# The fp6 layers' residual sum moves from VectorE to TensorE, and its copy out of PSUM to ScalarE

## The reference, cut to what matters

```python
x = x + 0.5 * _L1_ffn_ref(_layernorm(x, axis=-1), L1_ffn_weight, L1_ffn_bias)

# _L1_ffn_ref:
xq, xs = _mx_quantize(x2)          # blocks of 32 features share a scale; values go to the nearest of the fp6 grid
wq, ws = _mx_quantize(w2)
xd = (xq * xs[..., None]).reshape(x2.shape)
wd = (wq * ws[..., None]).reshape(w2.shape)
out = xd @ wd.T + bias
```

## Time and profile before

| what | value |
|---|---|
| median of three runs | 2520.27 us (2518.9 to 2527.7) |
| the profiled execution, its own time | 2511.65 us |
| span of its trace | 2509.8 us |
| TensorE, VectorE, ScalarE busy | 84%, 61%, 39% of the span |
| mean granted clock of TensorE | 0.916 |
| first fp6 stage | until 1623 us of the span |
| last fp6 stage | about 2408 to 2505 us |

### The profile page before, as it was taken

How to read it: one execution, slowest core, us unless ns; L and a number is a source line. 1 busy time by engine, 2 the same in 40 slices (tenths; PEclk the granted TensorE clock), 3 DMA queues, 4 the chain that set the end, 5 groups by cost and what they waited for, 6 DMA issues and landing times.

```text
span 2509.8 us, 38629 instructions
## 1 busy us (share of the span) xinstructions
PE 2113.4 (84%) x12842; PEld 1582.3 (63%) x12842; DVE 1519.2 (61%) x4411; ACT 970.8 (39%) x1961; POOL 319.6 (13%) x298
## 2 busy tenths in 40 slices
PE   5589999967999964899999647678998998999957
PEld 3478888855888944788888525524554554554446
DVE  7744344346555577444334498677777676777368
ACT  4122332222333342223233234325555555555643
POOL 4320000022000043300000252311001101100000
PEclk8799999988999997999999856769999999999976
DMA  8120101111000031200110130342242242242002
GB/s 264 43 65 25 31 27 31 31 51 40 1 1 1 1 110 45 72 25 27 31 31 27 54 92 7 75 53 58 40 53 53 52 52 52 53 52 28 2 9 67
DMA packets 84035, 114.83 MB, mean 46 GB/s; under 512 B 12212, under 2 KB 73816, under 8 KB 80728
## 3 DMA queue, kind: packets, MB, share of 16 engines
q1 hardware_dynamic: 77416, 94.80, 17.2%
q0 software_dynamic: 6432, 17.57, 2.2%
HBM read 69.16 MB, written 43.17 MB: 45 GB/s over the span
## 4 chain that ended last, share of the span: by engine, by line
PE 61%; DVE 26%; ACT 5%; issue 4%; DMA 2%; POOL 2%; DVEq 0%; ACTq 0%; SPq 0%; POOLq 0%
PE psum L775 10%; PE psum L777 10%; PE psum L776 10%; PE psum L126 5%; PE psum L2289 4%; PE psum L128 4%; PE psum L127 4%; DVE mt L2177 4%; PE psum L2268 3%; PE psum L862 3%; DVE m L2165 2%; PE psum L2248 2%; DVE m L2174 2%; DVE stats L160 2%; DVE xn L185 2%
## 5 line engine op out<-in xcount | busy, mean ns | idle before, releaser
L2128 ACT ACTIVATE pt<-psum 128x512 f32<-128x512 f32 (+3 forms) x768 | 333.7, 492 | 274.5 <-DVE psum L2203 180.7
L740 DVE SCALAR_TENSOR_TENSOR h<-psum,xg,sg 128x128 f32<-128x128 f32 x592 | 166.8, 344 | 415.4 <-PE psum L862 415.4
L556 ACT ACTIVATE sg<-psum 128x512 f32<-128x512 f32 x180 | 107.7, 598 | 573.8 <-PE psum L777 573.8
L775 PE MATMUL psum<-w_hi,xt_hi 128*128 (+1 forms) x720 | 285.1, 396 | 33.7 <-DVE xt_lo L705 33.7
L776 PE MATMUL psum<-w_lo,xt_hi 128*128 (+1 forms) x720 | 283.3, 393 | 0.0
L777 PE MATMUL psum<-w_hi,xt_lo 128*128 (+1 forms) x720 | 283.1, 393 | 0.0
L2248 PE MATMUL psum<-ks,qs 96*128 96x512 bf16 (+3 forms) x768 | 235.2, 346 | 34.3 <-DMA ks<-qk_scr 9.0
L2268 PE MATMUL psum<-qs,ks 99*128 99x512 bf16 (+3 forms) x768 | 238.7, 334 | 24.5 <-ACT pt L2128 18.8
L775 PE MATMUL psum<-w_hi,ht_hi 128*128 (+1 forms) x720 | 218.1, 303 | 0.2
L2272 PE MATMUL psum<-band,ident_r 128*128 128x256 f32 (+1 forms) x864 | 215.7, 338 | 0.0
L2177 DVE CUSTOM_DVE_ANT_0 mt<-psum,band_q 128x256 bf16<-128x256 f32 (+1 forms) x512 | 204.7, 400 | 17.3 <-PE psum L2248 7.1
(11 more groups left out here) (283 smaller groups left out, 4377.6 us busy)
## 6 DMA issues: line engine op xcount, KB each, us to landing
xg<-w_dram SPq DMA_DIRECT2D x54, 256.0 KB, 3.2
qk_scr<-parts SPq DMA_DIRECT2D x32, 384.0 KB, 2.5
qs<-qk_scr SPq DMA_DIRECT2D x96, 128.0 KB, 7.1
ks<-qk_scr SPq DMA_DIRECT2D x96, 128.0 KB, 7.7
xg<-rows_in SPq DMA_DIRECT2D x74, 132.0 KB, 2.1
rows_out<-yb SPq DMA_DIRECT2D x74, 128.0 KB, 1.7
x<-x_dram SPq DMA_DIRECT2D x4, 1024.0 KB, 8.5
out_dram<-x SPq DMA_DIRECT2D x4, 1024.0 KB, 4.5
```

What stands on the lines that cost most here:

```text
L740: ins = dve.scalar_tensor_tensor(out=h[i % 2][:, e, :], in0=u[:, e, :], scalar=xg[j % XSLOT][:, at:at + 1], in1=sg[i % 2][:, e, :], op0=AL ...
L775: pe.matmul(out, a[0], b[0], start=first, stop=False)
L2128: act.activation(pt[n % NPT][:, 0:q1 - q0], st_bank(n)[:, 0:q1 - q0], ACT.Exp).then_inc(*exped.up())
```

## The change

TensorE opens the accumulation of each tile with a matmul of the 128x128 identity by the tile of `X`, both in plain 32 bits, so that the residual is in the sum. The weight's two parts are halved as they are copied out of PSUM, and so is the row of ones that multiplies the bias. The sum in PSUM is then the new x, and ScalarE copies it into `X`, where VectorE had multiplied and added. The step `sum` keeps its place in the order and changes its engine.

```diff
+        W_SCALE = 0.5
...
-                    pool.memset(minus[:, :], -1.0).then_inc(*S("ones").up())
+                    pool.memset(minus[:, :], -W_SCALE).then_inc(*S("ones").up())
...
-                            act.activation(wt[0][:, c, :], ring.bank((kind, c))[:, 0:D],
-                                           ACT.Copy).then_inc(*wt_hi.up())
+                            act.activation(wt[0][:, c, :], ring.bank((kind, c))[:, 0:D], ACT.Copy,
+                                           scale=W_SCALE).then_inc(*wt_hi.up())
...
+                        elif kind == "sum":
+                            act.wait_ge(*lin(c + 1))
+                            act.activation(flat(X[:, c * TILES:(c + 1) * TILES, :]), ring.bank(("lin", c)),
+                                           ACT.Copy).then_inc(*lin_x.up())
...
-                            dve.tensor_tensor(wt[1][:, c, :], ring.bank((kind, c))[:, 0:D],
-                                              wt[0][:, c, :].bitcast(F32), ALU.subtract).then_inc(*wt_lo.up())
+                            dve.scalar_tensor_tensor(out=wt[1][:, c, :], in0=ring.bank((kind, c))[:, 0:D], scalar=W_SCALE,
+                                                     in1=wt[0][:, c, :].bitcast(F32), op0=ALU.mult,
+                                                     op1=ALU.subtract).then_inc(*wt_lo.up())
...
-                        elif kind == "sum":
-                            dve.wait_ge(*lin(c + 1))
-                            dst = flat(X[:, c * TILES:(c + 1) * TILES, :])
-                            dve.scalar_tensor_tensor(out=dst, in0=ring.bank(("lin", c)), scalar=0.5, in1=dst,
-                                                     op0=ALU.mult, op1=ALU.add).then_inc(*lin_x.up())
...
-                                pe.matmul(o, ones[:, :], bias_2[:, :], start=True, stop=False)
+                                pe.matmul(o, ident[:, :], X[:, c * TILES + t, :], start=True, stop=False)
+                                pe.matmul(o, ones[:, :], bias_2[:, :], start=False, stop=False)
```

## The result

The changed kernel takes 2531.2 us at the median of 20 runs (2522.8 to 2539.8), the kernel before 2520.1 us (2509.6 to 2529.1). The ratio is 1.0044, with an interval of 1.0029 to 1.0058: slower by 11 us, where +22 was forecast. The time lies in the forecast range; the size is half of it. The profiled execution took 2532.42 us, 20.8 more than that of before, so the profiled pair and the medians disagree by 10 us. That difference was the first thing to explain.

The account below looks back on a forecast made before the run. The prediction took TensorE at a mixed clock to become the last stage's bound, in place of VectorE and TensorE loops of nearly equal length. Last stage +11.3 and first +11.0 made +22.3 on the median 2520.3: 2543 us, range 2516 to 2572.

Parts of the forecast that it names:

- Sum: ... = +11.0 us: First fp6 stage: the terms of quads 0 to 7 and the stage's end together add 11.0 us.
- a first stage that ends within 4 us of its old time: First fp6 stage: a sign that the prediction, which added 11.0 us there, is wrong.
- the terms for quads 4 to 7 and the end: First stage after 1540 us: quads 4 and 6 +2.2 each, quad 5 +1.5, quad 7 +3.4, end +2.8.
- VectorE's wait for ScalarE's sums: First stage, quad 1: the longer product makes VectorE wait in the `collect` needing the sum, net +1.0 us (0.5 to 1.7).
- +11.3 us: Last fp6 stage: six quads at a mixed clock add 7.8 us, the last two quads 3.5.
- 12.0 us per quad: Last stage: TensorE bounds, its clock rising 7.5 us after a product's start; 12.0 us per quad against 10.70.
- The VectorE loop of a quad becomes 10.38 - 1.20 = 9.2 us: Last stage: without the two sums, 1.20 us on the chain, VectorE's loop per quad falls to 9.2 us.
- I take nothing: Last stage: ScalarE's added copy is covered by TensorE's transposes and costs nothing, 0.15 us at most per quad.
- The price of a product: Both fp6 stages: each identity product costs TensorE 0.44 us at the full clock, 0.86 at the half.
- The sum on the median: Whole kernel: +22.3 us, worked out on the profiled execution's 2511.65, is added to the median 2520.3.
- Rival B: Both fp6 stages: denser products hold the clock at 2.4 GHz, VectorE's saving decides; total -6, 2514 us; chance 0.12.
- Rival C: Both fp6 stages: the clock stays low throughout, 14.45 us per quad in the last; total +56, 2576 us; chance 0.15.

Follow-up runs that it names:

- first_only: The change in the first fp6 stage alone (TensorE adds twice the residual, ScalarE halves the sum), against the kernel before: ratio 1.0022 (1.0001 to 1.0043).
- before_third: The kernel before, unchanged, run once more for a third trace: 2527.1 us.
- last_only: The change in the last fp6 stage alone (TensorE adds twice the residual, ScalarE halves the sum), against the kernel before: ratio 1.0043 (1.0026 to 1.0060).
- after_full: The changed kernel with the bias product's two rows widened to 128 by zeros: ratio 0.9977 (0.9960 to 0.9995) to the kernel before.
- after_full_swap: The changed kernel with the bias product widened to 128 rows and, on VectorE, next quad's `scaled` ahead of this one's `even`: 2506.8 us, 0.9946 to the kernel before.
- no_ident: The changed kernel without the identity products, ScalarE still copying the sum: ratio 1.0021 (1.0003 to 1.0039) to the kernel before.
- double: The changed kernel with each identity product issued twice, counting the residual twice: ratio 1.0058 (1.0039 to 1.0077) to the kernel before.

## Why the prediction was wrong

It had the direction and the kind of loss; the size was twice what was measured. Point by point:

- *The first stage, "Sum: ... = +11.0 us", is the term that was mis-sized.* The traces give 3.7 us between the means, in a spread of 9 within the same code, and `first_only` 5.5 with an interval that ends short of 11. The forecast had named a first stage that ends within 4 us of its old time as a sign of being wrong; between the means it is met (the profiled pair has 4.9 us in length, 4.4 in its end). What failed is the part after 1540 us: the terms for quads 4 to 7 and the end, +12.1 in all. From quad 4's product to the end of the stage the four traces without the change took 64.3, 67.8, 71.1 and 72.2 us, the three with it 68.7, 69.7 and 69.7: +0.5 between the means. The terms took the clock of one execution, the shortest, as given and added the new products to it. From quad 4's product to quad 7's in the profiled execution of before, in `before_third` and in the changed kernel:

```profile
1559.10:1611.90 52.80, 39.74 (x195) 32.19 (x195) 37.39 (x65) 23.41 (x41) 15.60 (x10) 0.82 0.15 51
1561.70:1621.00 59.30, 46.07 (x195) 37.18 (x194) 37.34 (x65) 23.37 (x41) 15.58 (x10) 0.70 0.13 45
1559.10:1614.60 55.50, 43.69 (x220) 33.09 (x218) 33.73 (x59) 26.16 (x47) 16.24 (x11) 0.90 0.14 49
```

  From the first to the start of the last matmul, quads 4 and 6 took 5.3 and 5.4 us in the profiled execution, mostly at the upper clock, but 8.0 and 8.0 at the lower in `before_third` and `last_only`. With the change they took 7.0 to 7.1 and 6.6 in all three traces: 1.7 and 1.1 us more than in the execution shown, for the 2.2 priced, and less than in those two. Quad 7 was priced at +3.4 because its product ran at the half clock. In the profiled execution of the changed kernel:

```profile
1614.59 0.97 PE psum L1531 x2
...
1617.64 0.79 PE psum L1531 x2
...
1619.65 0.43 PE psum L1531 x2
...
1621.30 0.43 PE psum L1531 x2
...
1624.40 0.60 ACT v L1834
```

  The last tiles' products step by 0.43: the clock had risen, and the product took as long as without the added work, 1614.6 to about 1623 us against 1611.9 to 1620.3. In the other two traces it took 2.3 us more than before. Over the stage from its first bias DMA to its end the mean granted clock is 0.66, 0.63, 0.63 and 0.61 in the four traces without the change, 0.74, 0.70 and 0.70 in those with it. The other way, from the first product to quad 4's the stage took 77.4 us on the mean for 74.2, +3.2 where the terms had -1.0. There VectorE's wait for ScalarE's sums was priced for one quad; in the whole stage it came in four, 21.5 us with 10.5 at most, where before VectorE waited 7.3 us for the products in its sums. The end of the stage was right: 2.6 us for the 2.8 priced.
- *The last stage, "+11.3 us"*: measured 11.0 between the means of all traces, 10.8 by `last_only`. Here the total was right and its inside was not, so that it came out is in part luck. "12.0 us per quad" is the mean of the first six (13.7, 10.6, 13.3, 10.5, 13.3, 10.7), but by alternation: the clock rose only with the end of a slow quad's product, some 11 us after its start and not 7.5, and then held for one whole quad. The last two quads took 13.3 and 7.5, which is 8 more than in the profiled execution and 1 to 5 more than in the other three traces, for the 3.5 priced.
- *"The VectorE loop of a quad becomes 10.38 - 1.20 = 9.2 us" failed.* With TensorE out of the way (`after_full`) the loop was 10.5. Of the 1.2 us, 0.9 went to the wait for ScalarE's `sizes`, which the sums had covered; `after_full_swap` takes that wait away and gets 9.8 in its best quads.
- *"I take nothing" for ScalarE's copy failed.* I asked what it delays behind TensorE and not what it delays behind the `sizes`. `no_ident` puts the whole move at +5 us (ratio 1.0003 to 1.0039); how much of it is the copy alone was not measured.
- *The price of a product*, 0.44 and 0.86 us, was right: tiles of 2.94 us at the half clock, and in `double` 2.08 at the full, 0.44 over the changed kernel's 1.64.
- *The sum on the median.* I added a difference worked out on the profiled execution to a median 8.6 us above it. That execution had the shortest first and last stage of the four. Against it the changed kernel's profiled execution lost 16.1 us in the last stage and 4.9 in the first, 21.0 together, close to the 22.3 forecast but with both terms wrong in opposite directions. The median lost 11: part of the 22 is what other executions of the kernel before lose by themselves.
- *Rival B* did not occur, but `double` shows its mechanism a step away: there the upper clock held across the transposes and the gap of every quad, so what the prediction reads from its trace, that the clock falls when these come, isn't so in general. Rival C was wrong: four of eight quads ran at the upper level (only the first quad of `last_only` took the 14.4 us that C has for all). D was wrong by the record count.

Still open: how the first stage's few microseconds split into products, copies and clock, and whether the stages' 11.0 and 3.7 us or the median's 11.1 is nearer the truth. Three or four traces of each kind can't say: those of one kernel differ by 4 to 9 us in each stage. Why the clock rises early in one execution and late in another isn't shown either.

## What to carry to other kernels

Work taken off the busiest engine is worth only what does not cover another engine's work: look at what ran under the removed instructions, and whether the next one waits for it. Before moving work onto TensorE, look for a cheaper tile: a short weight operand among full ones cost more here than the whole change moved. Where a stage's time hangs on the granted clock, read several executions before taking a difference from one.

## What the runs showed of the hardware

- A matmul with two rows of weights among ones with 128 costs 0.51 us from end to end at 1.2 GHz and makes its successor cost 0.51, where each costs 0.21 with 128 rows (0.31 and 0.31 against 0.12 at 2.4 GHz). The 126 zero rows cost nothing that shows; the tile fell from 2.08 to 1.49 us. The Trainium skill, "TensorE: Matmul & The Clock Gate", section "LDWEIGHTS (loading the stationary operand)", says that a load of 32 rows takes as long as one of 128. The loads themselves bear this out roughly, 0.28 us for two rows and 0.33 for 128 at the half clock; what differs is that the two-row load starts with its own matmul and not under the one ahead of it.
- More matmul work went with a shorter stage: 85.4 us with two identity products a tile, 92.9, 92.9 and 89.2 with one, at a granted clock of 0.97 against 0.77, 0.77 and 0.80. With fewer products than either (`no_ident`) it was 0.58, and the wider bias product, which shortens the work, raised it too (0.65 at most to 0.73 without the identity, 0.80 at most to 0.84 with it).
